# Two attention layers with a gating scan in their gaps: the order within a step, and two elementwise operations given from GpSimd to VectorE

## The reference

```python
ek = exp(min(k, 30)); ekv = ek * v
# nf, df: forward scans of ekv, ek with a <- a * decay + e_t; nb, db: the same backward
euk = exp(min(u + k, 30))
num = nf + nb - ekv + euk * v
den = df + db - ek + euk
out = sigmoid(r) * num / max(den, 1e-8) * (0.8 + 0.2 * tf)
```

```python
attn = softmax(where(causal, -inf, q @ k.T / 4)); y = (attn @ v) @ Wo + bo
```

## Time and profile before

| | us |
|---|---|
| median of 3 runs | 744.61 |
| lowest and highest | 738.55, 745.58 |
| the profiled execution | 743.39 |
| its span, first to last instruction | 741.5 |

### The profile page before, as it was taken

The page is one execution under the profiler, slowest core; times in us unless marked ns, Lnnn a source line. Parts: engine busy times, 40 slices in busy tenths (PEclk is TensorE's granted clock), DMA queues, the critical chain, the costliest instruction groups (busy, mean ns, idle before and its releaser), DMA issues.

```text
span 741.5 us, 12279 instructions
## 1 busy us (share of the span) xinstructions
PE 542.3 (73%) x4564; PEld 417.7 (56%) x4564; DVE 444.5 (60%) x802; ACT 273.8 (37%) x557; POOL 255.2 (34%) x201
## 2 busy tenths in 40 slices
PE   0377985877751788858768557934999999999970
PEld 0255653544530455535545343533999999999960
DVE  4669686784958297876847287122655556665510
ACT  4235252542443344525423422102344444444430
POOL 2102111011102010110101007771477777777772
PEclk9999898998985799989989857986999999999995
DMA  8999500000000000000000043326498777868623
GB/s 300 252 218 249 132 1 1 2 1 1 1 1 1 0 2 1 2 1 2 2 1 1 1 149 114 118 101 226 127 219 221 204 195 189 203 192 211 155 25 62
DMA packets 56715, 71.96 MB, mean 97 GB/s; under 512 B 11777, under 2 KB 45036, under 8 KB 56544
## 3 DMA queue, kind: packets, MB, share of 16 engines
q1 hardware_dynamic: 40272, 57.48, 27.1%
q0 software_dynamic: 16400, 13.87, 9.9%
HBM read 42.22 MB, written 37.04 MB: 107 GB/s over the span
## 4 chain that ended last, share of the span: by engine, by line
PE 52%; DVE 20%; issue 10%; ACT 8%; POOL 7%; DMA 2%; POOLq 0%; SPq 0%; DVEq 0%; ACTq 0%
PE S L932 13%; PE PJ L945 7%; POOL xe_rows L396 5%; DVE negmax L1122 4%; PE OB L945 3%; ACT prob L483 3%; PE PJ L676 3%; PE S L744 3%; PE TB L917 3%; PE PJ L702 3%; PE S L740 3%; PE S L748 3%; PE PJ L714 2%; PE S L730 2%; PE S L726 2%
## 5 line engine op out<-in xcount | busy, mean ns | idle before, releaser
L932 PE MATMUL S<-xgT,wgu_s 128*128 128x384 f32 x576 | 108.6, 340 | 1.2 <-DVE hidden_f L1360 1.2
L1122 DVE TENSOR_REDUCE negmax<-S 128x4 f32<-128x512 f32 x64 | 58.2, 953 | 84.9 <-PE S L730 73.3
L483 ACT ACTIVATE prob<-S 128x1536 f32<-128x1536 f32 x32 | 46.4, 1452 | 148.2 <-PE S L748 148.2
L932 PEld LDWEIGHTS S<-xgT,wgu_s 128*128 128x128 f32 x576 | 99.3, 189 | 1.5 <-issue 1.4
L407 POOL DMA_INDIRECT out<-sig,y_token x48 | 75.1, 1565 | 47.5 <-ACT sig L650 35.0
L407 POOL DMA_INDIRECT odd_out<-sig,y_token x48 | 76.5, 1594 | 24.3 <-ACT sig L650 14.0
L345 POOL TENSOR_TENSOR eu<-eu,side 128x512 f32<-128x512 f32 x16 | 21.0, 1311 | 174.0 <-ACT eu L454 149.3
L355 POOL TENSOR_TENSOR nd<-both,eu 128x512 f32<-128x512 f32 x16 | 23.4, 1464 | 136.2 <-DVE both L1017 136.2
L396 POOL DMA_INDIRECT xe_rows<-x_tok,slot_i x48 | 47.3, 984 | 56.8 <-ACT x_tok L615 42.5
L945 PE MATMUL PJ<-x8m,hidden_f 128*128 128x256 f32 x256 | 60.5, 379 | 1.4 <-ACT sig L650 1.4
L945 PEld LDWEIGHTS PJ<-x8m,hidden_f 128*128 128x128 f32 x256 | 47.9, 190 | 6.7 <-issue 1.8
(11 more groups left out here) (178 smaller groups left out, 1078.7 us busy)
## 6 DMA issues: line engine op xcount, KB each, us to landing
xe_rows<-x8m SPq DMA_DIRECT2D x4, 3468.0 KB, 39.8
ratio<-xe_rows SPq DMA_DIRECT2D x32, 433.5 KB, 4.2
ek<-in_wgu SPq DMA_DIRECT2D x32, 384.0 KB, 4.8
x8m<-in_wd SPq DMA_DIRECT2D x32, 256.0 KB, 2.9
x<-in_x SPq DMA_DIRECT2D x1, 1024.0 KB, 6.4
odd_out<-x8m SPq DMA_DIRECT2D x1, 1024.0 KB, 28.2
out<-side SPq DMA_DIRECT2D x8, 128.0 KB, 5.2
out<-odd_out POOLq DMA_DIRECT2D x1, 1024.0 KB, 7.8
```

Of the source, the lines that this page charges most:

```text
L483: eng.activation(prob[:, v % 2, :, :], S[:, :, 0:3 * P], ACT.Exp).then_inc(sem(f"exp_{L}"), 1)
L932: ins = eng.matmul(S[:, m, 0:CAP], fast(wgu_s[:, j % 2, a, k, m * P:(m + 1) * P]), fast(xgT[:, j % 2, b, k, :]), start=n == 0, stop=n == N ...
L1122: ins = eng.tensor_reduce(negmax[:, v % 2, st, :, 0], S[:, :, cols], AX.X, ALU.max, negate=True)
```

## The change

POOL no longer makes the bonus product and the numerator's sum; DVE makes both in the odd step, between the scans and `refine` (and in the prologue for the first ratio). On PE, projections follow `turned_scores` and `neg_mm` instead of preceding `turned_scores`, but for the queries of batch 1, which stay; `y_mm` at u = 2 moves with them. On DVE, `residual` goes from the end of step u = 3 to just behind the maxima, and `scale_o` goes ahead of `denominator`. On ACT, `totals_inverse` goes ahead of `exps`, and `inverse` goes behind `o_out`.

```diff
@@ gpsimd
-            def bonus(b, n, buf):
...
-                eng.tensor_tensor(eu[:, buf, 1, :, :], eu[:, buf, 0, :, :], side[:, :, tok(b)], ALU.mult)\
-                   .then_inc(sem("bonus_made"), 1)
-            def numerator(n, buf):
...
-                eng.tensor_tensor(nd[:, 1, :, :], both[:, 1, :, :], eu[:, buf, 1, :, :], ALU.add)\
-                   .then_inc(sem("num_made"), 1)
...
-            attention(0)
...
-            attention(1)
@@ scalar
+                        if u == 0 and b:
+                            totals_inverse(L, b - 1, 1)
+                        if u == 2:
+                            totals_inverse(L, b, 0)
                         exps(L, v)
                         if v + 1 < B * QUADS:
                             neg_out(L, v + 1)
                         if u == 0 and b:
-                            totals_inverse(L, b - 1, 1)
-                        if u == 2:
-                            totals_inverse(L, b, 0)
-                        if ratio_now and u % 2 == 0:
-                            inverse(n)
-                        if u == 0 and b:
                             o_out(L, b - 1, 1)
                         if u == 2:
                             o_out(L, b, 0)
+                        if ratio_now and u % 2 == 0:
+                            inverse(n)
@@ tensor
                         if b == 0 and u == 2:
                             q_mm(L, 1)
-                        if b == 0 and u == 3:
-                            v_mm(L, 1)
-                        if 0 < b < B - 1:
-                            (q_mm, k_mm, None, v_mm)[u] and (q_mm, k_mm, None, v_mm)[u](L, b + 1)
-                        if b and u == 2:
-                            y_mm(L, b - 1)
                         turned_scores(L, v)
                         if v + 1 < B * QUADS:
                             neg_mm(L, v + 1)
-                        if b == 0 and u == 2:
-                            k_mm(L, 1)
+                        if 0 < b < B - 1 and u == 0:
+                            q_mm(L, b + 1)
+                        if 0 < b < B - 1 and u == 1 or b == 0 and u == 2:
+                            k_mm(L, b + 1)
+                        if b and u == 2:
+                            y_mm(L, b - 1)
+                        if b < B - 1 and u == 3:
+                            v_mm(L, b + 1)
@@ vector
+            def numerator(b, n, buf):
+
+                eng.wait_ge(sem("bonus_exp"), n + 1)
+                eng.tensor_tensor(eu[:, buf, 1, :, :], eu[:, buf, 0, :, :], side[:, :, tok(b)], ALU.mult)\
+                   .then_inc(sem("bonus_made"), 1)
+                eng.wait_ge(sem("bonus_made"), n + 1)
+                eng.wait_ge(sem("backward"), 2 * n + 2)
+                eng.tensor_tensor(nd[:, 1, :, :], both[:, 1, :, :], eu[:, buf, 1, :, :], ALU.add)\
+                   .then_inc(sem("num_made"), 1)
...
             scan_backward(0, 0, 1)
+            numerator(0, 0, 0)
             refine(0)
...
                             maxima(L, b * QUADS + u + 1)
+                        if u == 3 and b:
+                            residual(L, b - 1)
                         ratio_now = ratio_of(L, b, u)
+                        if ratio_now and u % 2 == 0:
+                            i, bb, n, buf = ratio_now
+                            bonus_arg(i, bb, n, buf)
+                            scan_forward(i, bb, n, buf, 0)
+                            scan_backward(n, buf, 0)
+                        if u == 0 and b:
+                            scale_o(L, b - 1, 1)
+                        if u == 2:
+                            scale_o(L, b, 0)
                         if ratio_now:
                             i, bb, n, buf = ratio_now
                             if u % 2 == 0:
-                                bonus_arg(i, bb, n, buf)
-                                scan_forward(i, bb, n, buf, 0)
-                                scan_backward(n, buf, 0)
                                 denominator(i, bb, n, buf)
                             else:
                                 scan_forward(i, bb, n, buf, 1)
                                 scan_backward(n, buf, 1)
+                                numerator(bb, n, buf)
                                 refine(n)
...
-                        if u == 0 and b:
-                            scale_o(L, b - 1, 1)
-                        if u == 2:
-                            scale_o(L, b, 0)
-                        if u == 3 and b:
-                            residual(L, b - 1)
```

More of the change, by code:

```diff
@@ L339, in _ @@
             eng.memset(decay_t[:, :, NC * T:NC * T + 1], 0.0).then_inc(sem("inner_made"), 1)
-            def bonus(b, n, buf):
-                eng.wait_ge(sem("bonus_exp"), n + 1)
-                settle(eng, "pool")
-                eng.tensor_tensor(eu[:, buf, 1, :, :], eu[:, buf, 0, :, :], side[:, :, tok(b)], ALU.mult)\
-                   .then_inc(sem("bonus_made"), 1)
-            def numerator(n, buf):
[L350 to L354, removed]
-                eng.tensor_tensor(nd[:, 1, :, :], both[:, 1, :, :], eu[:, buf, 1, :, :], ALU.add)\
-                   .then_inc(sem("num_made"), 1)
-            eng.wait_ge(sem("side_in"), 16)
-            bonus(0, 0, 0)
-            numerator(0, 0)
             eng.wait_ge(sem("amax_w"), 1)
```

## The result

| | before | after |
|---|---|---|
| median, us | 744.33 (4 runs) | 678.74 (4 runs) |
| lowest, highest | 738.55, 745.58 | 674.3, 679.37 |
| profiled execution, span | 743.39, 741.5 | 678.75, 676.9 |

The ratio is 0.912, with a 95% interval of 0.907 to 0.918. The changed kernel is faster by 64.6 us in the profiled executions, where 56.6 were forecast. Single runs of one kernel scatter by 4 us or more.

The account below looks back on a forecast made before the run. The prediction took waits for DVE's residual and the handover of tile S to bound the kernel. Savings of 26.4 (first layer), 21.2 (second) and 9.0 (ends) made 56.6 off 743.4: 687 us, range 676 to 712.

Parts of the forecast that it names:

- The long steps: At u=3 the value projection waits for DVE's residual, then runs slowly; the 6.67 us gaps and low clock go.
- TensorE's loop: Attention step from maxima to maxima on TensorE: 8.27 us with a projection, 7.53 without.
- DVE's loop: DVE's attention step: even at most 8.19 us, odd 7.84, with a gate 8.56, with the residual 8.71.
- the price of an added operation: Each operation moved to DVE takes 0.69 us, plus 0.03 for the pair's own wait; upper bound 1.64 each.
- The tightest place: ScalarE's even step: totals' inverse ends about 4.2 us behind the maxima, exponentials due at 4.28; no cost, 0.1 to spare.
- The step that gets worse: Batch 0, u=2: ScalarE's key copy slips some 0.8 us; step charged 14.06 instead of 13.26, the next 8.97.
- The sum: Twelve steps from the third maxima on, 106.4 us against 132.8; second layer, two steps more, 122.5 against 143.7.
- The ends: Last maxima to last output projection in each layer: 16.2 us against 20.72, 4.5 saved per layer.
- its reading of the even step: DVE's even step of 9.27 us loses POOL's stall of 1.08 and becomes at most 8.19, below 8.27.
- rival (a): DVE becomes the bound, stalls stay: even steps 9.27, odd 8.79; 709 us, or 712 with dear operations; chance 0.12.
- (b): The new order does not free the value projection; four gaps and slow projections stay, 34 us more, 721; chance 0.06.
- rival (c): Tensor clock falls to its lower level in attention steps, at most 6.4 us more per step, up to 841; chance 0.04.

Follow-up runs that it names:

- the two experiments: Changed kernel with DVE's residual back at the end of its step: 701.1 us; changed kernel with TensorE's projections back ahead of the turned scores: 692.9 us.
- the experiment: Changed kernel with ScalarE's inverse of the totals back behind the exponentials and the copy of the turned maxima: 698.3 us, ratio 0.941.
- The kernel with the order alone: Changed kernel with the bonus product and the numerator's sum back on POOL and off DVE: 682.2 us, ratio 0.915.
- the last kernel: Changed kernel with ScalarE's key projection copy first in batch 0, u = 2, and DVE's bonus product at the end of the even step: 669.9 us.

## Why the prediction was right, point by point

- **The long steps.** That the projection waits for a residual at the end of DVE's step, and that this costs twice, held: with the residual put back, the wait (3.83) and the slow projection (3.75 for 1.89) return. The prediction did not say how much of it each half of the order is worth; the two experiments do, 14.9 and 10.2 for 17.6.
- **TensorE's loop.** Forecast 8.27, measured 8.18. The term that was off is the projection, 1.83 by rows 3 and 1.73 behind the turn of the maxima (124.99 to 126.72). With some ten such steps in the two layers this is 1 of the 8 us by which the forecast fell short.
- **DVE's loop.** The stalls were POOL's: L970 is 0.162 to 0.166 in all 32 rows and L1010 0.69 in all 16, and the price of an added operation, 0.69, is what L998 and L1002 show (0.67, 0.69). The odd step measures 7.69 in batch 3 where it is alone (forecast 7.84), with a residual 8.47 and 8.35 (8.71), with a gate 8.55 (8.56); operations that don't wait for each other start 0.61 apart, not 0.72. The first step of batch 3 is 7.55, for which I had kept 8.19 with a wait in it that the new order takes away. The steps with a residual make 1.2 of the 8 us, the two of batch 3 in each layer 1.6.
- **The tightest place.** The totals' inverse ended 0.28 us ahead of the exponentials (123.88 + 0.42 to 124.58); the experiment shows that its place is worth 1.1 us in each even step.
- **The step that gets worse.** Rightly seen and mis-sized in the second layer: I charged 14.06 there, with a low clock, and it took 11.76, with the clock at 1.00 throughout; with the step behind it (8.55 for 8.97) this is 2.7 of the 8 us. The trace of the kernel before had the number: in its second layer the step took 285.31 - 273.75 = 11.56, at full clock behind a gap of 2.58. The sum took the first layer's 13.26 for both layers. The step did get worse, by 0.2 in the second layer and by 0.4 in the first (13.66), where 0.8 was charged.

```profile
273.75 1.82 DVE L1122 TENSOR_REDUCE negmax<-S 128x4 f32<-128x512 f32 x2
...
283.55 0.82 PE L726 MATMUL S<-causal_b,ident_b 128*128 128x384 bf16 x4 [2.58 <-ACT k_sb L527]
...
285.31 1.82 DVE L1122 TENSOR_REDUCE negmax<-S 128x4 f32<-128x512 f32 x2 [2.81 <-PE S L730]
```

- **The rest of the 8 us.** The ends came out as forecast, 16.24 for 16.2; the first layer's last projection then ran in 1.99 us and not 3.38, which I had not counted: 1.4. With 0.3 from the first layer's step at u = 2 and the one behind it these terms make up the 8 us. All were off to the same side, so that the time lies near the low end of the range.
- **What the move to DVE is worth.** The prediction gave it no price of its own, and its reading of the even step was too dear. It took the 9.27 as a loop in which only the stall of 1.08 would go; had the stalls stayed, each even step would have kept its 9.27, 1 us above TensorE's 8.27, as in rival (a). But 0.62 of the 9.27 was DVE's wait for the totals' inverse, which the new order takes away. With the stalls in place the even step is 8.42, 0.24 above TensorE's 8.18, and the stall of the odd step lies in a loop that TensorE's covers. So the move is worth close to nothing under this order: 682.2 without it and 678.7 with it, with intervals that overlap.

Rivals (a) and (b) had steps above 9 us and long steps of 17; in batches 1 to 3 of the trace no step is longer than 8.56. The clock, rival (c), stayed at 1.00 from 85 to 168 us and from 255 to 341.

## What to carry to other kernels

When two engines hand a tile back and forth, add up each engine's loop by itself, from start to start, and leave out the waits that the change takes away: what is moved within the shorter loop is worth next to nothing as long as that loop stays the shorter, and a wait inside the longer one costs all of its length and, on TensorE here, often the clock behind it. A step that occurs once in each layer is read in each layer. A producer that someone waits for belongs at the head of its engine's step, and a consumer behind the work that frees the shared tile; here it took both. An operation given to GpSimd can cost VectorE more than it would itself: 1.08 us of stall on an operation of 0.16, for a product that VectorE makes in 0.67.

## What was not expected of the hardware

The gap's length alone did not tell whether TensorE's clock fell. In the changed kernel it was at 0.50 behind a gap of 3.40 us in the first layer and at 1.00 behind one of 3.15 us in the second; in the kernel before it fell behind 2.99 us, less than that 3.15. The kernel with the order alone kept 1.00 behind a gap of 3.45 us at the same place of the first layer (71.56 to 75.01), and in the last kernel the clock read 0.50 from 219.90 to 222.90, while TensorE was busy, though the wait ahead of that work was only 1.95 us. DMA traffic does not tell the two first-layer gaps apart: its share was 1.09 in the one of 3.40 us and 1.10 in the one of 3.45. The runs here do not settle what else decides it.
